# Feed-forward stage of a two-layer attention kernel: the statistics of a group's first row tile, and the load of its rows, stand earlier

## The reference, cut to what matters

```python
x = x + xattn(layernorm(x), ctx, ctx, mask)          # band of 128 keys each way, 4 x 1024 rows of 512
y = layernorm(x)
for l in range(2):
    h = shift_token(y)                               # second half of the columns comes from the row before
    q, k, v = split(h @ wqkv[l]); q, k = rotary(l2norm(q) * qs, l2norm(k) * ks)
    y = y + local_attention(q, k, v) @ wo[l]         # 8 heads, window 256
    h = shift_token(y)
    h = (h - h.mean(-1)) / sqrt(h.var(-1) + 1e-5) * ln_g[l] + ln_b[l]
    a, g = split(h @ w1[l] + b1[l])                  # 512 -> 2 x 1365
    y = y + (a * gelu(g)) @ w2[l] + b2[l]            # 1365 -> 512
out = x + y
```

## Time and profile before

| what | value |
|---|---|
| time, median of 3 runs | 2922.42 us (2921.98 to 2922.68) |
| the profiled execution's own time | 2922.74 us |
| its span | 2920.9 us |
| PE busy (matmul) | 2878.8 us, 99% of the span |
| DVE busy | 2078.8 us, 71% |
| ACT busy | 1341.0 us, 46% |
| POOL busy | 1337.9 us, 46% |
| DMA engines, mean rate | 187 GB/s |

### The profile page before, as it was taken

The page is one execution under the profiler, slowest core; times in us unless marked ns, Lnnn a source line. Parts: engine busy times, 40 slices in busy tenths (PEclk is TensorE's granted clock), DMA queues, the critical chain, the costliest instruction groups (busy, mean ns, idle before and its releaser), DMA issues. The chain is left out here.

```text
span 2920.9 us, 53018 instructions
## 1 busy us (share of the span) xinstructions
PE 2878.8 (99%) x20256; PEld 2526.5 (86%) x20256; DVE 2078.8 (71%) x4135; ACT 1341.0 (46%) x2807; POOL 1337.9 (46%) x1406
## 2 busy tenths in 40 slices
PE   9999999999999999999999999999999999999999
PEld 7887878888889999999998887878888999999998
DVE  8977777776677666766657767777676766666765
ACT  7875656565554222222235555655554322222221
POOL 7757677676642211122205677776662222222221
PEclk9999999999999999999999999999999999999999
DMA  6753233322157777777683223332127777777775
GB/s 219 239 184 100 94 109 101 117 91 80 37 186 282 262 267 267 266 259 256 255 312 115 94 93 107 109 116 91 51 73 280 268 273 271 270 279 280 276 274 187
DMA packets 184897, 547.02 MB, mean 187 GB/s; under 512 B 26678, under 2 KB 82490, under 8 KB 162116
## 3 DMA queue, kind: packets, MB, share of 16 engines
q1 hardware_dynamic: 184500, 543.57, 52.5%
q10 hardware_dynamic: 144, 0.07, 0.0%
HBM read 447.11 MB, written 93.70 MB: 185 GB/s over the span
## 5 line engine op out<-in xcount | busy, mean ns | idle before, releaser
L1246 PE MATMUL quad<-fhT_f,slot_f 128*128 128x256 f32 (+1 forms) x2088 | 597.6, 286 | 0.2 <-DVE sums_f L2060 0.2
L1247 PE MATMUL quad<-fhT_f,slot_f 128*128 128x256 f32 (+1 forms) x2088 | 589.8, 282 | 0.0
L1248 PE MATMUL quad<-fhT_f,slot_f 128*128 128x256 f32 (+1 forms) x2088 | 589.7, 282 | 0.0
L1246 PEld LDWEIGHTS quad<-fhT_f,slot_f 128*128 128x128 f32 (+1 forms) x2088 | 392.2, 188 | 2.8 <-DVE sums_f L2060 0.8
L1665 ACT ACTIVATE gate_f_raw<-gate_f_raw,bias_f 128x512 f32<-128x512 f32 (+1 forms) x176 | 127.2, 723 | 580.5 <-DVE gate_f_raw L2083 580.5
L1247 PEld LDWEIGHTS quad<-fhT_f,slot_f 128*128 128x128 f32 (+1 forms) x2088 | 392.6, 188 | 0.0
L1248 PEld LDWEIGHTS quad<-fhT_f,slot_f 128*128 128x128 f32 (+1 forms) x2088 | 392.5, 188 | 0.0
L1533 ACT ACTIVATE lprob<-lprob,small 128x384 f32<-128x384 f32 (+2 forms) x512 | 288.5, 565 | 179.0 <-DVE small L1884 179.0
L2168 POOL TENSOR_SCALAR stats<-stats 128x1 f32<-128x1 f32 x64 | 43.5, 680 | 701.6 <-DVE stats L2023 701.0
L2285 POOL TENSOR_TENSOR turned_qk<-with_cos,with_sin 128x256 f32<-128x256 f32 x252 | 186.8, 762 | 337.0 <-DVE with_sin L1908 243.6
L1000 PE MATMUL bank_pair<-wqkv_h,hT 128*128 128x512 f32 x992 | 318.7, 402 | 0.0
(11 more groups left out here) (296 smaller groups left out, 7286.4 us busy)
## 6 DMA issues: line engine op xcount, KB each, us to landing
slot_f<-parts SPq DMA_DIRECT2D x160, 1792.0 KB, 7.5
slot_f<-parts SPq DMA_DIRECT2D x16, 1190.0 KB, 5.3
s_in<-stream SPq DMA_DIRECT2D x128, 128.0 KB, 2.9
s_res<-stream SPq DMA_DIRECT2D x64, 256.0 KB, 2.9
stream<-a_out SPq DMA_DIRECT2D x64, 256.0 KB, 2.0
res_f<-stream SPq DMA_DIRECT2D x63, 256.0 KB, 7.4
h_in_f<-stream SPq DMA_DIRECT2D x112, 128.0 KB, 5.2
parts<-part_high SPq DMA_DIRECT2D x20, 512.0 KB, 2.6
```

The lines of the kernel that those rows point to most:

```text
L1246: e.matmul(bank[0:n, :], high, row_high, start=c == 0, stop=False)
L1247: e.matmul(bank[0:n, :], high, row_low, start=False, stop=False)
L1248: ins = e.matmul(bank[0:n, :], low, row_high, start=False, stop=c == 1)
```

## The change

Three edits.

1. `moments` of the first row tile of a group, tile `(g + 2) * GROUP` as seen from group `g`, moves on DVE from block 0 of group `g + 1` to the end of the short block of group `g`, behind `split_u`. `normalise` of that tile stays in block 0.
2. For the first group of a layer there is no group before it: there the statistics of tile `GROUP` move from block 0 to the end of `attend(l)`, behind `make_u(l, 0, 0)` and ahead of the last `add_residual`.
3. The load of those rows moves on SP from block 9 to block 6.

```diff
                     if g + 1 < GROUPS and j in (0, 2, 4) and (g, j) > (0, 0):
                         ffn_load(l, (g + 1) * GROUP + j // 2 + 1)
-                    if g + 2 < GROUPS and j == 9:
+                    if g + 2 < GROUPS and j == 6:
                         ffn_load(l, (g + 2) * GROUP)
...
                         make_u(l, 0, 0)
+                        moments(l, GROUP)
                     if d and ended and s != TILES - 1:
                         add_residual(tail)
...
                     if g + 1 < GROUPS and j in (0, 2, 4, 6):
-                        moments(l, (g + 1) * GROUP + j // 2)
+                        if j:
+                            moments(l, (g + 1) * GROUP + j // 2)
                         normalise(l, (g + 1) * GROUP + j // 2)
+                    if g + 2 < GROUPS and j == FULL:
+                        moments(l, (g + 2) * GROUP)
```

## The result

| | before | changed |
|---|---|---|
| median of 4 runs (us) | 2922.55 (2921.98 to 2923.11) | **2905.34** (2905.07 to 2905.7) |
| profiled execution: own time, span (us) | 2922.74, 2920.9 | 2905.07, 2903.3 |

The ratio is 0.994, 95% interval 0.9928 to 0.9952: faster by 0.6%. The prediction said 2904.8 us.

The account below looks back on a forecast made before the run. PE, 99% busy, bounds the kernel, so DVE acts only through PE's gaps. 14 groups x 1.26 = 17.6 us off the median of 2922.42 gives 2904.8 us; own range 2902.5 to 2907, with most of the first rival 2902.5 to 2910.

Parts of the forecast that it names:

- The place: PE's transposes in block 2 wait for ACT's first_f, made late by DVE; 14 of 16 waits are of this kind.
- The worth on PE: Waiting in each block 2, from block lengths: 12.17 - 10.49 - 0.42 = 1.26 us a group, all to go.
- The lead: DVE reaches add_first of block 1 earlier by 0.94 (statistics) + 0.74 (wait for POOL) = 1.68 us.
- The short block: The moved statistics pair takes 0.94 us on DVE there, hidden; cost between nothing and 0.1 us a group.
- the margin: In the short block, DVE could start add_third of block 0 1.34 us earlier; any excess passes to block 1.
- The first groups: Two groups: a_out 0.41 us later, add_first of block 1 1.27 earlier, just about covering PE's wait; gain 1.26 each.
- The load: Two DMAs of rows on SP, issued three blocks earlier, some 24 us: no cost, no gain.
- What is late next: DVE was in step at block 3 with 0.30 us to spare; nothing given back, later blocks move by 1.26.
- Only the pair counts: Rival: scaling step still waits for POOL; chain leads by 0.94, gain about 0.85 us a group, 2910.5 us; chance 0.07.
- the pause: DVE's 0.79 us wait for POOL inside normalise in block 0; its going was to save 0.74 us.
- Given back: Rival: in blocks 3 to 10 PE meets another late engine or weight slot, ending as before, 2922 us; chance 0.05.
- Slower: Rival: DVE waits in the short block for rows; slower from 3.0 us late, about 2944 us at 5; chance 0.03.

Follow-up runs that it names:

- e3: Changed kernel with POOL's steps for the first tile held back until split_u of block 0, so the pause inside normalise returns: 2909.66 us.
- e4: Changed kernel with an idle copy of the statistics pair (BN_STATS and BN_AGGR, result unused) in block 0, where the pair stood: 2912.66 us.
- e5: Changed kernel with two idle statistics pairs behind the moved one in the short block: 2908.23 us.
- e1: Kernel before with only the load of the first tile's rows moved from block 9 to block 6: 2923.04 us beside 2922.92.
- e2: Changed kernel with the load of the rows back in block 9: 2905.2 us.
- e7: Changed kernel with four idle statistics pairs behind the moved one in the short block: 2930.76 us.

## Why the prediction was right

**The place.** PE's wait for `first_f` was the gap that DVE could close, 14 times. It went 14 times, and the time with it.

**The worth on PE**, 1.26 a group, read from block lengths and not from the 0.78 of idle time: 1.25 in twelve groups, 1.36 in the two first ones, where the block before had not been looked at and is 12.29 and not 12.17. 17.7 for the 17.6 of the sum. Had the 12.6 us of the list of waits been taken, the sum would have been near 11. The reason given for the difference between 1.26 and 0.78, that a matmul after a wait is slow to start, holds for 0.05 of it only. 0.25 were the short waits ahead of the transposes, which the prediction named too, and the rest is that the record of the matmul ahead, 0.28, covers 0.16 of a gap that is counted from a step of 0.12.

**The lead**, 0.94 + 0.74 = 1.68: measured 1.69, and each part by itself (0.94 in e3, 0.75 in e4).

**The short block.** The pair costs 0.85 there and not 0.94 (1117.41 to 1118.26): the instruction behind it does not read what the BN_AGGR writes, does not wait for it, and starts 0.14 after it does, where the centring step started 0.22 after it. So the margin was 1.43 and not 1.34. It is hidden: add_third has kept its 0.82 of waiting. That the pair might be stretched beside POOL was the upper end, 0.1 us a group. It was not stretched. The Trainium skill (SBUF — State Buffer, "Who interferes with whom") says that a DVE instruction with at most one SBUF input does not contend with GpSimd. The rows here agree on both sides: two of the moved BN_STATS ran beside a residual addition of POOL, at 945.54 and 2295.68, and took their 0.68, while the two-input steps took 1.37 instead of 0.69 (`split_u` at 2294.39) and, in e5, 1.48 instead of 0.75. What the prediction left out is that these steps stand in the same short block and take their stretch out of the same margin. POOL's own first step takes 190 ns in 14 more cases now (22 instead of 8), where the centring step no longer runs beside it.

**The first groups.** `a_out` was to move to 863.79 and `add_first` to start 1.27 earlier. They came at 863.41 and 866.66. All of this stretch runs 0.27 us earlier than in the kernel before (`u_f` at 861.90 for 862.17), so `a_out` moved by 0.30 and `add_first` came 868.37 - 866.66 - 0.27 = 1.44 earlier: the pair was again shorter than taken. What was put at "just about" covered it. The fourth weight slot was issued at the same instant as before, and no wait came of it.

**The load**: no cost, no gain, shown by e1 and e2. **What is late next**: nothing; blocks 3 to 10 kept their lengths, except the slot's block with 0.3.

**The rivals.** *Only the pair counts*, 2910.5, would have been right had the pause stayed: e3 is 2909.66. *Given back* fell with 0.74 to spare at block 3. *Slower* is real, and the bound on it held: beyond margin and lead (3.0 us of extra time in the short block) the kernel is slower, and 3.72 gave 2930.76. It is shown for more work in the block, though; no run made the rows late. What the prediction had wrong in it is the place: PE stands in block 1 first, for the buffer that `add_first` frees. Three idle pairs, 2.77, cost most of the gain but not all of it.

## What to carry to other kernels

When an engine off the bound comes late once in a period, look on it for work whose inputs were there long before, and for a pause in which it waits for its own result to come back from another engine; moving the first step of such a round trip a stage ahead takes both off the chain. Price it by the difference in length of whole blocks with and without the wait, and find the amount that suffices: earlier than the bounding engine needs is worth nothing. Before the work is put into another stage, read there how long the next instruction waits for the bounding engine, and who needs a buffer from the instructions that it pushes back.

## What was not expected of the hardware

- A lateness of PE of 0.25 us (e3) has no entry among its waits, as the record of the matmul ahead of it lasts 0.28 while matmuls follow each other at 0.12. Fourteen blocks with 0.31 or more were over 4 us of that kernel. The 0.78 us of idle time in the earlier trace rows was 0.95 of lateness.
- What stands behind a BN_AGGR of 0.18 us on DVE starts 0.10 to 0.14 after it does when DVE's program has no wait there, and 0.22 after it when it waits for the BN_AGGR to be done: the centring step, which reads its result, and whatever follows an idle pair, whose helper waits for its own end. e7 has both in one place: a BN_AGGR at 1122.42 with the next BN_STATS at 1122.52, and one at 1123.22 with the next at 1123.44. So a pair costs 0.81 to 0.86 in the one case and some 0.94 in the other, and the one that moved went from the second to the first.
- POOL's step on 128x1 elements takes 190 ns alone, 0.62 in e3 where it starts 0.17 into the centring step (1126.46 and 1126.29), and 0.75 where both start together: it seems to be let in only when that step ends.
